# The first tile's loads, sent one kind at a time

## The chip, the cores and the metric

The kernel runs on one core of one Trainium2 chip. The metric is the device time of one execution in microseconds (us), the median of several runs. The kernel before took 1606.19 us (three runs, 1605.28 to 1607.11).

## The reference

The input is 16 sequences of 512 tokens with 256 features, in float32. Each token is normalised (`xn`), and two branches read `xn`: a linear attention with 16 heads, and a gated feed-forward network (FFN) with ternary weights. Both are added to the input.

```python
xn = layernorm(x)
# attention
q, k, v = split(xn @ W_qkv.T + b_qkv)
q, k = elu(q) + 1, elu(k) + 1
out = (q @ (k.T @ v)) / clip(q . sum(k), 1e-6)
attn = layernorm(out @ W_proj.T + b_proj) * gamma + beta + xn
# FFN, hidden width 1024; every weight is -1, 0 or 1, with one scale per row
h = silu(lin(xn, w1)) * lin(xn, w2)        # "gate" and "up"
h = gelu(lin(h, h1)); h = gelu(lin(h, h2))
return x + attn + lin(h, w3)
```

## The kernel before

A tile is one sequence, 512 tokens by 256 features. There are 16 tiles, one after the other, and all weights stay in SBUF from the first tile on. A matmul on float32 data is made of several matmuls on a high and a low part: three for the attention's weights (`three`, lines 388 to 393), two for the ternary FFN weights (`products`, line 379). The order of work on every engine is written out by hand. `over_tiles` runs `prologue` once, for what the first tile needs before its main part, then `body` for each tile; a body also does the prologue's steps for the next tile. So only the first tile's prologue has nothing beside it.

The loads ahead of the first tile are sent by three engines:

- SyncE (`sp`): the tile `x` (512 KB, line 296), then the bias of k and v (256 KB broadcast, line 326), the FFN's scales and the bias of q (`vec`, 17 KB, line 327), four more row vectors (512 KB, line 328), and then the first piece for the weight check (176 KB, line 306). The check looks at all FFN weights in 64 pieces, to learn whether they are as simple as assumed.
- ScalarE (`act`): the constants (`const`, 132 KB: an identity matrix and masks), the qkv weights (`wqkv_raw`, 768 KB), the projection's weights (`wproj_raw`, 256 KB), at lines 593 to 595.
- GpSimd (`pool`): the FFN weights in six pieces (`load_weights`, line 346). Piece 0 is gate and up (2 MB), 1 to 4 the two hidden layers (2 MB each), 5 the output layer (1 MB). Before piece 0 GpSimd waits until `x` has landed (`x_loaded`); pieces 1 to 5 follow behind the first tile's `ln1`.

The way to the first matmul with real data in the first tile is this. When `x` is there, VectorE takes its statistics (`ln1_stats`, line 708) and GpSimd computes the inverse root of the variance (`inverse_root`, line 353, one instruction). VectorE normalises (`ln1_apply`, line 714), TensorE transposes `xn` (line 401), ScalarE makes the high part (line 627) and VectorE the low part (line 727). The qkv weights are split too: ScalarE makes the high part (line 598) as soon as they have landed, and VectorE the low part (line 850), which stands behind `ln1_apply` and ahead of line 727 on VectorE. Then TensorE makes q, k and v (`q_step`, `kv_step`, lines 391 to 393) and goes on to gate and up in `body` (line 386). Before all that it does five warm-up products on zeros (line 377, ten matmuls in the profile).

ScalarE waits for `vec` after its line 598. TensorE waits for `const` before the first transposes, for `s_w[0]` at the first gate group, and for `s_w[1]` and `s_w[2]` in the first hidden group.

Of the kernel before, what the change touches and what calls it, by code (L numbers as in the profile page):

```python
# [98 lines left out]
def block_kernel(nc, H, w_ffn, w_attn, vecs, rows, consts, out):  # L99
# [70 lines left out]
    def sem(name):  # L170
        return nc.alloc_semaphore(name)
# [5 lines left out]
    s_qkv_raw = sem("qkv_weights_loaded")  # L177
# [3 lines left out]
    s_w = [sem(f"ffn_weights_loaded_{i}") for i in range(len(w_pieces))]  # L181
# [13 lines left out]
    x_loaded = Count(sem("x_loaded"), 1, unit=16)  # L195
# [77 lines left out]
    def over_tiles(eng, first, prologue, body):  # L273

        prologue(first)
        with eng.Fori(first, first + B - 1) as t:
            body(t, True)
        body(first + B - 1, False)

    def second_pass_if_needed(eng, run):  # L280
        eng.wait_ge(s_flag, 1)
        need = eng.value_load(flag[0:1, 0:1])
        with eng.If(need != 0):
            run()

    block = nc.Block()
    with block:


        @block.sync  # L290
        def _(sp):
            sp.sem_inc(acc_free.sem, 1)

            def load_x(t, first):
                sp.wait_ge(acc_made.sem, acc_made.at(t - 1, TC - 1))
                sp.dma_start(x[:], of_tile(x_dram, t - first)).then_inc(x_loaded.sem, 16)

            def of_tile(dram, tile):
                return dram[tile] if isinstance(tile, int) else dram[bass.ds(tile, 1)][0]

            def body_of(first):
                def load_piece(t, j):
                    sp.wait_ge(piece_checked.sem, piece_checked.at(t, j - 1))
                    col = (t * CHECKS + j) * CHECK_COLS
                    src = w_ffn[:, col:col + CHECK_COLS] if isinstance(col, int) else w_ffn[:, bass.ds(col, CHECK_COLS)]
                    sp.dma_start(raw[:], src.bitcast(U32)).then_inc(piece_loaded.sem, 16)

                def body(t, more):
                    if first == 0:
                        load_piece(t, 0)  # L310
                    if more:
                        load_x(t + 1, first)
                    if first == 0:
                        for j in range(1, CHECKS):
                            load_piece(t, j)
                    for half in range(2):
                        two = slice(2 * half, 2 * half + 2)
                        sp.wait_ge(out_made.sem, out_made.at(t, half))
                        sp.dma_start(of_tile(out_dram, t - first)[:, two], acc[:, two]).then_inc(out_stored.sem, 16)
                    sp.wait_ge(out_stored.sem, out_stored.at(t, 1))  # L320
                    sp.sem_inc(acc_free.sem, 1)
                return body

            def prologue(t):
                load_x(t, 0)
                sp.dma_start(rowv[:, R_BKV:], rows[:, R_BKV:].to_broadcast([P, 2 * D])).then_inc(s_bias_kv, 16)
                sp.dma_start(vec[:], vecs).then_inc(s_vec, 16)
                sp.dma_start(rowv[:, :R_BKV], rows[:, :R_BKV].to_broadcast([P, R_BKV])).then_inc(s_rows, 16)

            over_tiles(sp, 0, prologue, body_of(0))  # L330

            def second():
                sp.dma_start(w_full[:], w_ffn).then_inc(s_reload, 16)
                over_tiles(sp, B, lambda t: load_x(t, B), body_of(B))
            second_pass_if_needed(sp, second)


        @block.gpsimd
        def _(pool):
            nc.gpsimd.memset(ones[:], 1.0).then_inc(s_ones, 1)  # L340
            nc.gpsimd.memset(power[:], -0.5).then_inc(s_power, 1)
            pool.wait_ge(x_loaded.sem, x_loaded.at(0, 0))

            def load_weights(i):
                lo, hi = w_pieces[i]
                pool.dma_start(w[:, lo:hi], w_ffn[:, lo:hi]).then_inc(s_w[i], 16)

            load_weights(0)
            pool.wait_ge(s_power, 1)

            def inverse_root(t, var, done):
                pool.wait_ge(var.sem, var.at(t, 0))
                nc.gpsimd.tensor_tensor(rstd[:], vare[:], power[:], ALU.pow).then_inc(done.sem, 1)  # L353

            def ln1(t):
                inverse_root(t, ln1_var, ln1_rstd)

            def body(t, more):
                inverse_root(t, ln2_var, ln2_rstd)
                if more:  # L360
                    ln1(t + 1)

            def prologue(t):
                ln1(t)
                for i in range(1, len(w_pieces)):
                    load_weights(i)

            over_tiles(pool, 0, prologue, body)
            second_pass_if_needed(pool, lambda: over_tiles(pool, B, ln1, body))

# [219 lines left out]

        @block.scalar
        def _(act):
            act.dma_start(const[:], consts).then_inc(s_const, 16)
            act.dma_start(wqkv_raw[:].rearrange("p k n -> p (k n)"), w_attn[:, 0:DC * 3 * D]).then_inc(s_qkv_raw, 16)
            act.dma_start(wproj_raw[:].rearrange("p k n -> p (k n)"), w_attn[:, DC * 3 * D:]).then_inc(s_proj_raw, 16)
# [402 lines left out]
```

## Time and profile before

| | |
|---|---|
| median of three runs | 1606.19 us |
| span of the profiled execution, first to last instruction | 1605.2 us |
| TensorE busy with matmuls | 1591.0 us (99%) |
| VectorE busy | 945.4 us (59%) |
| ScalarE busy | 527.6 us (33%) |
| GpSimd busy | 38.1 us (2%) |

The trace comes from one execution of its own. Its span leaves out what lies around the first and the last instruction; the median of the runs is 1.0 us above it. In the profile, PE is TensorE's matmuls and PEld its weight loads, DVE is VectorE, ACT ScalarE, POOL GpSimd and SP SyncE. A name with a q behind it (ACTq) is an engine's instruction queue, which issues the transfers. L12 is line 12 of the kernel.

### The profile page before, as it was taken

Reading aid. Unit: us, or ns where it says so; the run is one execution under the profiler, and the core shown is the slowest. Engines: PE = TensorE matmul, PEld = TensorE weight load, DVE = VectorE, ACT = ScalarE, POOL = GpSimd, SP = SyncE. Lnnn points to the kernel's source line nnn. Section 1 sums busy time; section 2 is a strip of 40 time slices with the busy share of each in tenths; the row PEclk is TensorE's granted clock in tenths of the full one; section 3 lists DMA queues with packets and bytes.
Section 4 is the critical chain, followed back from the end, with each engine's and each line's share of the span. In section 5 each row is a group of like instructions: output and inputs, shape, how many; then the busy total and the mean of one; then the engine's idle time right before and its main releaser. Section 6 shows DMA issues by size and latency. Waiting matters only on the chain.

```text
span 1605.2 us, 22443 instructions
## 1 busy us (share of the span) xinstructions
PE 1591.0 (99%) x7884; PEld 1326.0 (83%) x7884; DVE 945.4 (59%) x1927; ACT 527.6 (33%) x817; POOL 38.1 (2%) x44
## 2 busy tenths in 40 slices
PE   8999999999999999999999999999999999999998
PEld 5888888888888888888888888888888888888886
DVE  5656657466564656647566474664746646566563
ACT  3324142241423424233242332423324143241421
POOL 1000000000000000000000000000000000000000
PEclk9999999999999999999999999999999999999999
DMA  9000000000000000000000000000000000000000
GB/s 355 23 12 11 27 18 22 11 11 27 18 22 18 4 27 18 22 22 0 27 18 27 18 9 18 18 27 18 18 9 18 27 18 22 11 11 27 18 10 20
DMA packets 28114, 42.07 MB, mean 26 GB/s; under 512 B 2112, under 2 KB 26816, under 8 KB 27328
## 3 DMA queue, kind: packets, MB, share of 16 engines
q1 hardware_dynamic: 26800, 29.12, 5.7%
q0 software_dynamic: 864, 11.53, 1.8%
q10 hardware_dynamic: 432, 1.18, 0.2%
q8 instruction: 10, 0.16, 0.0%
q14 instruction: 8, 0.07, 0.0%
HBM read 33.44 MB, written 8.39 MB: 26 GB/s over the span
## 4 chain that ended last, share of the span: by engine, by line
PE 99%; DMA 0%; DVE 0%; POOL 0%; issue 0%; DVEq 0%; POOLq 0%
PE ps L386 74%; PE ps L519 7%; PE ps L391 4%; PE ps L392 4%; PE ps L393 4%; PE ps L442 2%; PE ps L431 2%; PE ps L452 1%; PE ps L401 1%; DMA x<-in_H 0%; DVE wqkv_parts L850 0%; DVE xn L714 0%; DVE bn_stats L708 0%; POOL rstd L353 0%; DVE xn L837 0%
## 5 line engine op out<-in xcount | busy, mean ns | idle before, releaser
L386 PE MATMUL ps<-hidden_a,w_ffn 128*128 128x512 f32 x2048 | 488.1, 397 | 0.0
L386 PE MATMUL ps<-hidden_b,w_ffn 128*128 128x512 f32 x2048 | 484.4, 396 | 0.0
L386 PEld LDWEIGHTS ps<-hidden_b,w_ffn 128*128 128x128 f32 x2048 | 383.5, 188 | 91.6
L386 PEld LDWEIGHTS ps<-hidden_a,w_ffn 128*128 128x128 f32 x2048 | 381.4, 188 | 88.5
L622 ACT ACTIVATE value_ring<-ps,vectors 128x512 f32<-128x512 f32 x256 | 173.1, 689 | 693.7 <-PE ps L386 684.4
L386 PE MATMUL ps<-xnT,w_ffn 128*128 128x512 f32 x1024 | 249.4, 398 | 0.0
L386 PEld LDWEIGHTS ps<-xnT,w_ffn 128*128 128x128 f32 x1024 | 190.1, 188 | 43.6
L803 DVE CAST hidden_a<-value_ring 128x512 fp32r<-128x512 f32 x128 | 54.5, 426 | 216.0 <-ACT value_ring L622 216.0
L789 DVE SCALAR_TENSOR_TENSOR value_ring<-ps,vectors,gate_ring 128x512 f32<-128x512 f32 x128 | 94.2, 746 | 83.5 <-ACT gate_ring L604 83.5
L519 PEld LDWEIGHTS ps<-w_ffn,hidden_a 128*128 128x128 f32 x1024 | 123.9, 188 | 2.9
L519 PE MATMUL ps<-w_ffn,hidden_a 128*128 128x256 f32 x1024 | 124.6, 279 | 0.0
L803 DVE CAST hidden_b<-value_ring 128x512 fp32r<-128x512 f32 x128 | 54.5, 425 | 113.6 <-ACT value_ring L622 113.3
L604 ACT ACTIVATE gate_ring<-ps,vectors 128x512 f32<-128x512 f32 x128 | 86.7, 689 | 99.2 <-PE ps L386 99.0
L805 DVE TENSOR_TENSOR hidden_b<-value_ring,hidden_b 128x512 fp32r<-128x512 f32 x128 | 88.6, 692 | 4.4
L805 DVE TENSOR_TENSOR hidden_a<-value_ring,hidden_a 128x512 fp32r<-128x512 f32 x128 | 88.6, 692 | 4.4
L794 DVE TENSOR_TENSOR hidden_a<-value_ring,hidden_a 128x512 fp32r<-128x512 f32 x128 | 87.4, 683 | 2.2
L609 ACT ACTIVATE hidden_a<-value_ring 128x512 fp32r<-128x512 f32 x128 | 80.0, 625 | 9.7 <-DVE value_ring L789 9.7
L639 ACT ACTIVATE exp_tmp<-zkv 128x256 f32<-128x256 f32 x64 | 26.8, 418 | 150.1 <-DVE zkv L739 150.1
L845 DVE SCALAR_TENSOR_TENSOR low_bits<-raw_weights,low_bits 128x352 uint32<-128x352 uint32 x64 | 33.5, 523 | 68.7 <-DMA raw_weights<-in_w_ffn 68.7
L353 POOL TENSOR_TENSOR rstd<-var_plus_eps,power 128x4 f32<-128x4 f32 x32 | 34.3, 1072 | 1503.1 <-DVE var_plus_eps L703 1503.1
L739 DVE TENSOR_TENSOR zkv<-ps,row_vectors 128x512 f32<-128x512 f32 x64 | 44.3, 692 | 22.4 <-PE ps L393 22.4
L837 DVE TENSOR_TENSOR xn<-ps,row_vectors 128x512 f32<-128x512 f32 x32 | 22.1, 692 | 49.3 <-PE ps L519 49.3
(76 smaller groups left out, 1338.8 us busy)
## 6 DMA issues: line engine op xcount, KB each, us to landing
raw_weights<-in_w_ffn SPq DMA_DIRECT2D x64, 176.0 KB, 2.3
w_ffn<-in_w_ffn POOLq DMA_DIRECT2D x5, 2048.0 KB, 14.0
x<-in_H SPq DMA_DIRECT2D x16, 512.0 KB, 3.6
out_dram<-acc SPq DMA_DIRECT2D x32, 256.0 KB, 2.2
w_ffn<-in_w_ffn POOLq DMA_DIRECT2D x1, 1024.0 KB, 24.6
wqkv_raw<-in_w_attn ACTq DMA_DIRECT2D x1, 768.0 KB, 5.5
row_vectors<-in_rows SPq DMA_DIRECT2D x1, 512.0 KB, 7.8
wproj_raw<-in_w_attn ACTq DMA_DIRECT2D x1, 256.0 KB, 6.8
```

Source lines behind the costliest of these rows:

```text
L386: r = mm(bank, a, b, start=first and part == 0, stop=last and part == 1)
L391: mm(bank, wl, xh, start=first, stop=False)
L392: mm(bank, wh, xl, start=False, stop=False)
L393: return mm(bank, wh, xh, start=False, stop=last)
L519: r = mm(pair_bank(g, j)[:, 0:D], f(a) if full else a, wk, start=k == 0 and part == 0, stop=k == HC - 1 and part == 1)
L604: nc.scalar.activation(gate[:, o % 2, :], pair_bank(o, 0), ACT.Silu, scale=vec[:, V_GATE + o:V_GATE + o + 1]).then_inc(silu_made.sem, 1)
L609: nc.scalar.activation(ha[:, o, 0, :], val[:, o % 2, :], ACT.Copy).then_inc(gate_hi.sem, 1)
L622: nc.scalar.activation(val[:, n % 2, :], pair_bank(g, j), ACT.Gelu, scale=vec[:, col:col + 1]).then_inc(gelu_made.sem, 1)
L789: v.scalar_tensor_tensor(out=val[:, o % 2, :], in0=pair_bank(o, 1), scalar=vec[:, V_UP + o:V_UP + o + 1], in1=gate[:, o % 2, :], op0=ALU.m ...
L794: v.tensor_tensor(ha[:, o, 1, :], val[:, o % 2, :], ha[:, o, 0, :].bitcast(F32), ALU.subtract).then_inc(split.sem, 1)
L803: v.tensor_copy(dst[:, o, 0, :], val[:, n % 2, :]).then_inc(hid_hi.sem, 1)
L805: v.tensor_tensor(dst[:, o, 1, :], val[:, n % 2, :], dst[:, o, 0, :].bitcast(F32), ALU.subtract).then_inc(split.sem, 1)
```

## The change

Three waits are added and one is replaced. SyncE and ScalarE wait until `x` has landed before they send anything else. GpSimd waits for the qkv weights (`s_qkv_raw`) where it waited for `x`, before it sends piece 0; and it waits until piece 0 has landed before it sends pieces 1 to 5. Sizes and places of the transfers stay the same, and no computing instruction is added or moved.

```diff
             def prologue(t):
                 load_x(t, 0)
+                sp.wait_ge(x_loaded.sem, x_loaded.at(t, 0))
                 sp.dma_start(rowv[:, R_BKV:], rows[:, R_BKV:].to_broadcast([P, 2 * D])).then_inc(s_bias_kv, 16)
@@
             nc.gpsimd.memset(power[:], -0.5).then_inc(s_power, 1)
-            pool.wait_ge(x_loaded.sem, x_loaded.at(0, 0))
+            pool.wait_ge(s_qkv_raw, 16)
@@
             def prologue(t):
                 ln1(t)
+                pool.wait_ge(s_w[0], 16)
                 for i in range(1, len(w_pieces)):
                     load_weights(i)
@@
         def _(act):
+            act.wait_ge(x_loaded.sem, x_loaded.at(0, 0))
             act.dma_start(const[:], consts).then_inc(s_const, 16)
```

## Rows read from the trace of the kernel before

**Rows 1.** The page: the span, and TensorE's share.
```profile
span 1605.2 us, 22443 instructions
PE 1591.0 (99%) x7884; PEld 1326.0 (83%) x7884; DVE 945.4 (59%) x1927; ACT 527.6 (33%) x817; POOL 38.1 (2%) x44
```

**Rows 2.** Who waited for whom, whole span: us in total, times, longest.
```profile
PE ps L401 <- DVE xn L714: 3.8, 1, 3.8
...
PE ps L377 <- DVE value_ring L691: 2.6, 1, 2.6
...
PE ps L391 <- DVE xnT L727: 1.1, 1, 1.1
```

**Rows 3.** The chain that ended last, 0 to 47 us: start, us, what.
```profile
1.20 7.40 DMA x<-in_H
...
10.83 0.10 issue
10.93 1.04 POOL rstd L353
12.00 1.38 DVE xn L714 x4
13.38 1.67 DVE wqkv_parts L850
15.05 0.66 DVE xnT L727
...
15.84 0.76 PE ps L391
...
21.30 0.43 PE ps L391
...
21.97 0.23 PE ps L393
```

**Rows 4.** The timeline, 0 to 28 us: start, us, instruction, idle before.
```profile
0.75 0.39 ACTq L593 DMA_DIRECT2D constants<-in_consts  x1
...
1.18 0.45 ACTq L594 DMA_DIRECT2D wqkv_raw<-in_w_attn  x1
...
1.69 0.51 SPq L326 DMA_DIRECT2D row_vectors<-in_rows  x1
...
6.67 1.48 ACT L598 ACTIVATE wqkv_parts<-wqkv_raw 128x1536 fp32r<-128x1536 f32 x1 [3.17 <-DMA wqkv_raw<-in_w_attn]
...
8.70 1.40 DVE L708 BATCH_NORM_STATS2 bn_stats<-x 128x6 f32<-128x256 f32 x4 [5.82 <-DMA x<-in_H]
...
8.90 0.71 POOL L346 DMA_DIRECT2D w_ffn<-in_w_ffn  x1 [8.01 <-DMA x<-in_H]
...
11.94 2.83 POOL L346 DMA_DIRECT2D w_ffn<-in_w_ffn  x5
```

**Rows 5.** Transfers, whole span: size each, median us from issue to landing.
```profile
x<-in_H SPq DMA_DIRECT2D x16, 512.0 KB, 3.6
...
w_ffn<-in_w_ffn POOLq DMA_DIRECT2D x1, 1024.0 KB, 24.6
wqkv_raw<-in_w_attn ACTq DMA_DIRECT2D x1, 768.0 KB, 5.5
row_vectors<-in_rows SPq DMA_DIRECT2D x1, 512.0 KB, 7.8
...
constants<-in_consts ACTq DMA_DIRECT2D x1, 132.0 KB, 2.3
```

**Rows 6.** The same view, 8.5 to 10 us: piece 0 alone.
```profile
w_ffn<-in_w_ffn POOLq DMA_DIRECT2D x1, 2048.0 KB, 7.8
```

**Rows 7.** The timeline again: the first users of the other loads.
```profile
14.37 1.08 ACT L627 ACTIVATE xnT<-ps 128x512 fp32r<-128x512 f32 x2 [6.22 <-PE ps L401]
...
27.00 3.89 PE L386 MATMUL ps<-xnT,w_ffn 128*128 128x512 f32 x16
...
45.47 7.71 PE L386 MATMUL ps<-hidden_a,w_ffn 128*128 128x512 f32 x32
```

## The prediction

> **What bounds the kernel now.** I read the page first. TensorE is busy for 1591.0 of 1605.2 us [rows 1], so it is idle for 14.2 us in all, and only time before its first real product, idle time, or time at its lower clock can be gained by sending loads otherwise. The view of who waited for whom, over the whole span, has three waits of TensorE that are not weight loads: 2.6 us before the warm-up, 3.8 us for `xn` and 1.1 us for the low part of `xnT` [rows 2]. All three lie before 16 us. No wait of TensorE on a transfer is in that list: gate and up, the hidden layers and the output layer were each there when they were wanted. So as long as none of them comes late now, the change can only matter through the stretch up to 15.84 us, where the first q product starts [rows 3]. From there TensorE runs without a gap until its last product, and whatever shifts this start shifts the end.
>
> The chain of waits shows what sets the 15.84 [rows 3]. `x` is issued at 1.20 and lands at 8.60. VectorE's statistics end at 10.78 (after them stands 0.10 of issue, at 10.83), GpSimd's inverse root runs from 10.93, the normalising from 12.00, the low part of the qkv weights from 13.38, the low part of `xnT` from 15.05 to 15.71, and TensorE starts 0.13 later. The reader is to see that `x` is the late transfer here, and that the qkv weights are not: issued at 1.18 [rows 4], they took 5.5 us [rows 5] and were there at 6.7, when ScalarE took them up [rows 4], long before VectorE came to them at 13.38.
>
> **`x` alone.** The first `x` took 7.40 us [rows 3], beside the constants, the attention's weights and the row vectors. The median of all 16 `x` loads is 3.6 us [rows 5], and 15 of them meet almost no traffic. With nothing else sent, `x` should land at 1.20 + 3.6 = 4.8, some 3.8 us sooner. The statistics need 8.70 to 10.83, so they would end near 7.0. If that were all, the start of q would move up by 3.8 us.
>
> **The qkv weights behind `x`.** They can no longer overlap with it. ScalarE resumes when `x` is there: the lag from landing to first instruction was 0.10 us on VectorE (8.60 to 8.70) and 0.30 on GpSimd (to 8.90) [rows 3, 4]; I take 0.1. The constants' issue is first, and the weights' issue starts 0.43 after it (0.75 to 1.18) [rows 4]: 4.8 + 0.1 + 0.43 = 5.35. For the transfer I take its own row, 5.5 us [rows 5]. They had `x` (512 KB) and the row vectors beside them then, and will have the two row vectors (256 and 512 KB), `vec` and the check's first piece beside them now, so it is the nearest case. Landing: 10.9, where it was 6.7. The bounds are wide. Below, a smaller transfer with little beside it, `x` at 3.6, gives 9.0. Above, the 512 KB of row vectors that took 7.8 us in the crowd [rows 5] give 13.2.
>
> **GpSimd's wait for the qkv weights.** This is the step that decides. The inverse root of the first tile stands behind piece 0 on GpSimd, and piece 0 now waits for the qkv weights. Before, GpSimd was through with its issue (8.90 + 0.71 = 9.61) before the variance was there [rows 4]. Now the variance is ready at 7.0 and lies there until the weights have landed. Call that landing T. Then: lag 0.3, issue 0.71 [rows 4], 0.10 to the next instruction, taken from the row of issue [rows 3]: the inverse root starts at T + 1.1. From its start to the start of q the chain has 15.84 - 10.93 = 4.91 us of steps that stay as they are [rows 3]: the root, normalising, both low parts. So q starts at T + 6.0. It starts as before if T is 9.8. With T = 10.9 it starts at 16.9, that is 1.1 us later than 15.84. At the bounds: 15.0 (0.8 sooner) and 19.2 (3.4 later). The gain on `x` is given away in full, for the reason that everything behind GpSimd's wait starts with the qkv weights.
>
> ScalarE's high part of the weights takes 1.48 us from T [rows 4], and is done when VectorE wants it, at T + 1.1 + (13.38 - 10.93) = T + 3.55. That step hides, and with it a table load of ScalarE if that should fall behind the same wait.
>
> A rule that bears on this: the Trainium skill, in DMA: Bandwidth & Descriptors (Anatomy of one DMA, SWDGE path), gives a transfer from GpSimd as about 2.0 us plus its bytes over 436 GB/s. That would be 3.8 us for 768 KB, and by it T would be 9.2 and q would start 0.6 us sooner than before. The `x` row agrees roughly, since the rule gives 3.2 us and the trace has 3.6 [rows 5]; these two transfers are sent by other engines, though, and the weights are not alone. It is the case of the first rival below.
>
> **SyncE's wait.** Queued behind it are the k and v bias, `vec`, the other row vectors and the check's first piece. The bias now goes at 4.9 instead of 1.69, everything behind it by the same 3.2 us. The slowest of this group took 7.8 us [rows 5]. So `vec`, issued near 5.5 (the bias' issue takes 0.51 [rows 4]), is there by 13.3; ScalarE wants it before its line 627, at 14.37 [rows 7] and now at 15.4. The bias is there by 12.7 and wanted behind the q products, which start after 15.0 even at the lower bound; the rest is wanted later still in VectorE's order. The constants, sent at 4.9 and 2.3 us on the way [rows 5], are wanted by the transposes near 14.7. Cost nothing, with 2.1 us of cover for `vec` at the least. The cover shrinks if T is early: at T = 9.0 ScalarE wants `vec` at 13.5.
>
> **Piece 0.** It is issued at 11.2 instead of 8.90. Its row has 7.8 us [rows 6], with less beside it now, since pieces 1 to 5 are held back: landing by 19.0. TensorE wants it at 27.00 [rows 7], now 28.1. Cost nothing, 9 us of cover.
>
> **GpSimd's wait for piece 0.** The five issues start at 19.3 instead of 11.94 [rows 4]. Behind them on GpSimd stands only the inverse root of the second layernorm, which follows the first hidden groups. The last of the five was issued at 11.94 + 2.83 - 0.55 = 14.2 and landed 24.6 us later [rows 4, 5], at 38.8, so 26.9 after the first issue, and part of that was spent on piece 0. So all five are in by 46.2. The first hidden group wants only piece 1, at 45.47 [rows 7] and now 46.6. Cost nothing.
>
> **The clock.** TensorE's matmuls of 512 columns come every 0.43 us until 21.30 and every 0.23 from 21.97 [rows 3]: the lower and the higher level, 1.2 and 2.4 GHz. The rise came 5.8 us after the start of q. The clock is down because of the idle time before, and that gap of 3.8 us [rows 2] only grows, so nothing more is lost there. If the rise follows the work, the delay of 1.1 us stays whole. If it comes at the same moment as before, 2.5 matmuls that would have run at the lower level run at the higher one, and the delay is 2.5 x 0.23 = 0.6. If it came later still, each us would add about 0.5 us. The Trainium skill, in TensorE: Matmul & The Clock Gate (the HAM clock gate), says that the monitor runs freely and does not start with the kernel, so that the moment of rise differs from run to run. By that rule the mean delay over many runs is the whole 1.1; one trace can't show it.
>
> **Sum.** `x` 3.8 sooner; the weights and GpSimd's wait turn that into a start 1.1 us later; everything else hides. The profiled execution would go from 1605.2 to 1606.3. The median lies 1.0 above the span, so I forecast 1606.19 + 1.1 = 1607.3. About 0.2% (3.2 us) is what a measurement of this kernel can tell from no change; this is a third of it.
>
> **The rivals.**
>
> 1. The qkv weights come faster than their old row, since `x` is no longer beside them, T = 9.0 to 9.8. For it: `x` was sent at the same time as they were (1.20 and 1.18 [rows 3, 4]) and is twice the size of the bias that is sent at their side now. Against: the row vectors are sent at the same moment. Time: 0.8 us sooner, 1605.4. Chance 0.2.
>
> 2. The row vectors take more from the weights than `x` did, being sent together with the constants, ahead of the weights. T = 12 to 13.2, 2.2 to 3.4 later, 1608.4 to 1609.6. Chance 0.12. Against it: the weights came through ahead of their neighbours before (5.5 against 7.8 us for fewer bytes [rows 5]).
>
> 3. The first `x` is slow of itself (start of the queue, first access), and not because of its neighbours: it lands at 8.6 as before, and the weights follow. ScalarE sends them at 9.15, T is 14.65, q starts at 20.7, 4.8 us later: 1611.0. It is slower by over 0.2% from T = 13.0 on, so from a landing of `x` at 6.9. For it speaks that the first `x` has the longest time of the 16. Against it, the constants, sent before it, landed in 2.3 us [rows 5], so the start costs less than that. Chance 0.05.
>
> 4. Piece 0 becomes the wait, because its place in the order is later. It would have to take 16.9 us and took 7.8 [rows 6]. If it took the 24.6 of the last piece, TensorE would stand for 7.7 us more: 1615. Chance 0.02.
>
> 5. The waits act otherwise than the diff says, for example the start stays where it was: 1606.2. Chance 0.03.
>
> **Chances and range.** The forecast (T from 9.8 to 12, a delay of 0 to 2.2 us) has 0.58, the rivals 0.2, 0.12, 0.05, 0.02 and 0.03. The forecast and rival 2 up to 1609.2 and most of rival 1 make 8 in 10, with the three runs of before themselves 1.8 us apart; the range is 1605.0 to 1609.2. Slower by over 0.2% are rivals 3 and 4 and the end of rival 2: 0.08. Faster by over 0.2% would need T = 6.6, which not even the lower bound gives: 0.01. Within: 0.91.
>
> **What would show it.** In the profile of the changed kernel: `x` lands near 4.8 (right) or later than 6.9 (rival 3). The qkv weights land near 10.9, with GpSimd's wait before line 346 put down to them and not to `x`. The inverse root starts 1.1 us behind that landing, though its input is ready near 7.0. The q product starts near 16.9. Pieces 1 to 5 are issued after 18, and the list of TensorE's waits has no transfer in it. The clock's rise is at 21 to 23. The forecast is wrong if q starts before 15.8, if a wait of TensorE on `w_ffn` shows, or if `vec` or the constants end ScalarE's or TensorE's wait.

## The result, and the profile after

The changed kernel took 1608.95 us (median of 18 runs, 1607.81 to 1610.32), the kernel before 1605.81 us (18 runs, 1604.43 to 1607.11) beside it. The ratio is 1.002, with a 95% interval of 1.0013 to 1.0027: 3.1 us slower, and some 2.1 to 4.3 by the interval. I had forecast 1.1 us slower. The direction and the part of GpSimd's wait were right; the qkv weights took 2.1 us longer than I had taken them to. The size was nearly three times what I gave, and lies at the edge of the 0.2% that I had called hard to tell from nothing. In the experiments below two executions of the kernel before took 2633 and 4067 us, and no ratio counts them.

The page after. TensorE's busy time has grown by 0.7 us, and the clock's mean in the first slice is lower; the other 2.2 of the 2.9 us of span are time in which TensorE stands still.

```profile
span 1608.1 us, 22443 instructions
PE 1591.7 (99%) x7884; PEld 1326.7 (82%) x7884; DVE 945.5 (59%) x1927; ACT 527.3 (33%) x817; POOL 38.0 (2%) x44
```

The chain that ended last, 0 to 34 us (start, us, what). It answers to [rows 3].

```profile
1.19 3.32 DMA x<-in_H
4.54 0.39 ACTq L596
4.96 7.56 DMA wqkv_raw<-in_w_attn
...
13.64 1.05 POOL rstd L354
14.72 1.39 DVE xn L717 x4
16.11 0.25 issue
16.36 1.10 PE ps L403 x4
17.55 0.61 ACT xnT L630
18.18 0.70 DVE xnT L730
18.88 0.14 issue
19.02 0.76 PE ps L393
...
24.47 0.39 PE ps L393
24.86 0.24 PE ps L394
```

The reader is to see three things. `x` lands at 4.51 instead of 8.60. The chain then leaves `x` and runs through the qkv weights, which take 7.56 us, and from them over GpSimd to the inverse root. And the chain has changed its members behind the root: where it went through the low part of the weights on VectorE, it now goes through the transposes (line 403), ScalarE and then VectorE. q starts at 19.02 instead of 15.84, 3.2 us later.

The waits, whole span (us in total, times, longest), against [rows 2]: VectorE now waits 8.0 us for the root, whose input has been ready since 6.7.

```profile
POOL w_ffn L347 <- DMA wqkv_raw<-in_w_attn: 11.9, 1, 11.9
...
DVE xn L717 <- POOL rstd L354: 8.0, 1, 8.0
...
PE ps L403 <- DVE xn L717: 6.7, 1, 6.7
```

The transfers in the first 110 us (size, median us to landing) answer to [rows 5]. The constants take 5.2 us where they took 2.3.

```profile
wqkv_raw<-in_w_attn ACTq DMA_DIRECT2D x1, 768.0 KB, 7.6
...
row_vectors<-in_rows SPq DMA_DIRECT2D x1, 256.0 KB, 4.8
...
constants<-in_consts ACTq DMA_DIRECT2D x1, 132.0 KB, 5.2
```

From the start of q on nothing differs up to the last computing instruction: gate and up start at 30.17 instead of 27.00, and VectorE's last instruction ends at 1603.19 instead of 1600.02, both 3.2 us later. The spans differ by 2.9, so 0.3 us is made up behind that, where only the output is still being stored.

### The profile page after: what moved, and what is told of

It reads as the page before. It is cut to its first block, busy times and chain, and to the rows that moved or that the text cites. A ratio compares the mean times of both kernels' runs of the same rounds, so it can differ in the third digit from the quotient of the medians.

```text
span 1608.1 us, 22443 instructions
## 1 busy us (share of the span) xinstructions
PE 1591.7 (99%) x7884; PEld 1326.7 (82%) x7884; DVE 945.5 (59%) x1927; ACT 527.3 (33%) x817; POOL 38.0 (2%) x44
## 4 chain that ended last, share of the span: by engine, by line
PE 98%; DMA 1%; DVE 0%; issue 0%; POOL 0%; ACT 0%; ACTq 0%; DVEq 0%; POOLq 0%
PE ps L388 74%; PE ps L521 7%; PE ps L393 4%; PE ps L394 4%; PE ps L395 4%; PE ps L444 2%; PE ps L433 2%; PE ps L454 1%; PE ps L403 1%; DMA wqkv_raw<-in_w_attn 0%; DMA x<-in_H 0%; DVE xn L717 0%; POOL rstd L354 0%; DVE xnT L730 0%; DVE xn L840 0%
```

## Experiments

Twelve kernels were run; the question was why the qkv weights take 7.6 us, and what of the loss is GpSimd's order. The times of most are within a few us of each other, and single executions of the kernel before differ by more than 2 us, so for the runs with one execution I read the trace and draw nothing from the time. In the table, "consts" and "weights" are us from issue to landing, "landed" and "q" the moments at which the qkv weights were there and the first q product started. The kernels with a ratio were timed against the kernel before in several rounds. There is one trace of each kernel. Where the loads beside the weights are the same, the weights' time repeats: 7.56, 7.51 in the changed kernel and e2, and 4.45, 4.34 and 4.50 in e1, e3 and e8.

| kernel | consts | weights | landed | q | ratio to before (95%) |
|---|---|---|---|---|---|
| before | 2.3 | 5.5 | 6.7 | 15.84 | |
| changed | 5.2 | 7.56 | 12.52 | 19.02 | 1.002 (1.0013 to 1.0027) |
| e1 rows behind weights | 2.3 | 4.45 | 9.43 | 15.47 | 0.9996 (0.9987 to 1.0005) |
| e2 root first | 5.1 | 7.51 | 12.56 | 16.60 | 1.0003 (0.9994 to 1.0012) |
| e3 both | 2.2 | 4.34 | 9.47 | 13.52 | 0.998 (0.9971 to 0.9989) |
| e4 spread rows of the weights first | 5.1 | 6.90 | 11.85 | 18.35 | |
| e5 even 256 KB of H first | 3.0 | 7.25 | 12.29 | 18.79 | |
| e6 512 KB behind | 5.4 | 7.42 | 12.57 | 19.07 | |
| e7 bias behind | 2.3 | 6.03 | 11.13 | 17.63 | |
| e8 both, and filler | 2.2 | 4.50 | 9.63 | 13.68 | 0.9974 (0.9963 to 0.9984) |
| e9 only 256 KB of H beside | 3.2 | 5.08 | 10.11 | 16.61 | |
| e10 only one row of H beside | 4.5 | 6.00 | 11.16 | 17.65 | |
| e11 SyncE's and ScalarE's waits alone | 5.0 | 8.82 | 13.99 | 18.04 | 1.0017 (1.0007 to 1.0027) |
| e12 GpSimd's waits alone | 2.2 | 5.7 | 6.9 | 16.48 | 1.0004 (0.9994 to 1.0014) |

### The two costs taken out one by one (e1, e2, e3)

The edit of e1 to the changed kernel, on SyncE:

```diff
                 sp.wait_ge(x_loaded.sem, x_loaded.at(t, 0))
-                sp.dma_start(rowv[:, R_BKV:], ...)   # the bias
                 sp.dma_start(vec[:], vecs).then_inc(s_vec, 16)
+                sp.wait_ge(s_qkv_raw, 16)
+                sp.dma_start(rowv[:, R_BKV:], ...)
```

> SyncE sends `vec` behind `x`, and everything else only when the qkv weights have landed. All else as in the changed kernel. Theory A (the 256 KB bias, one row of 2 KB read for all 128 partitions, holds the DMA engines while the constants and the qkv weights stand behind it): the constants land in under 3 us, the qkv weights in about 4.5 us instead of 7.6, near 9.5; q starts at that landing + 6.0 to 6.5, near 15.5 to 16; 3 us faster than the changed kernel, level with the kernel before (1605.8, +-0.7). Theory B (a load that is sent after a wait is slow of itself, the queue has to start again): the qkv weights still take over 7 us, q starts near 19, 1609.

Its chain, 0 to 24 us:

```profile
1.19 3.34 DMA x<-in_H
...
4.98 4.45 DMA wqkv_raw<-in_w_attn
...
10.55 1.05 POOL rstd L355
...
15.47 0.77 PE ps L394
```

The weights took 4.45 us and landed where theory A had them; theory B, that a load sent after a wait is slow of itself, is out. q starts 3.5 us sooner than in the changed kernel, and the kernel is level with the one before. So taking away what SyncE sends beside the weights is enough to win back what was lost. It is not the only way: e2, next, comes back to the same level without it.

The edit of e2 to the changed kernel, on GpSimd:

```diff
-            pool.wait_ge(s_qkv_raw, 16)
-            load_weights(0)
@@ prologue
                 ln1(t)
+                pool.wait_ge(s_qkv_raw, 16)
+                load_weights(0)
                 pool.wait_ge(s_w[0], 16)
```

> GpSimd does the first inverse root before it waits for the qkv weights and sends piece 0. All else as in the changed kernel. Theory A: the root starts near 6.7 instead of 13.6; the qkv weights land at 12.5 as before; from there the high part 1.5, the low part 1.7, the low part of xnT 0.7, so q starts near 16.6, 2.4 us sooner than in the changed kernel: 1606.6. The transposes run right behind the warm-up, at the higher clock. Rival: the order on GpSimd costs nothing, since the weights' split sets the start anyway: q near 19, 1609.

Its chain. The root is gone from it, and the weights' own split sets the start:

```profile
5.05 7.51 DMA wqkv_raw<-in_w_attn
...
12.59 1.49 ACT wqkv_parts L601
...
14.10 1.76 DVE wqkv_parts L853
15.86 0.61 DVE xnT L730
...
16.60 0.76 PE ps L393
```

With the weights as slow as in the changed kernel, q starts 2.4 us sooner, at 16.60 as expected to the tenth. GpSimd's order alone costs those 2.4 us, 4.0 us from landing to q against 6.5.

e3 has both edits.

> Both edits together: SyncE's rows behind the qkv weights, and GpSimd's root first. Theory A: weights land near 9.5, q starts 4.0 us later, near 13.5, over 2 us sooner than in the kernel before: 1603.5, and less if the clock is still high. Rival: `vec` comes late (ScalarE waits for it ahead of the high part of xnT) or something else now ends last, and q starts near 15 to 16: 1605 to 1606. Theory B: q near 16.5, 1606.5.

q started at 13.52, and the median was 1603.3 us against 1606.42 of the kernel before: a real gain, whose interval reaches from 1.8 to 4.7 us. So the plan of the change, `x` first and the rest in the order of need, does pay once the row vectors stand behind the weights and the root ahead of the wait.

### What SyncE's loads do to the weights (e4 to e7, e9, e10)

First, 256 KB from 128 rows of the attention's weights were put in the bias' place, with the bias behind `vec`. They land in `acc`, so SyncE now declares `acc` free only when they are there; those lines are left out here and in the next edits shown:

```diff
+                sp.dma_start(acc[:]...[:, 0:2 * D], w_attn[:, 0:2 * D]).then_inc(s_probe, 16)
                 sp.dma_start(vec[:], vecs).then_inc(s_vec, 16)
                 sp.dma_start(rowv[:, R_BKV:], ...)   # the bias
```

> The changed kernel with a load added where the bias stood: 256 KB from 128 different rows of HBM, packets of 2 KB as the bias has, into a tile that is not in use yet; `vec` and the bias follow. So 256 KB more are sent, and nothing else changes. Theory A (it is the one row read for all that is slow): the added load's packets take about 0.08 us each instead of 0.19, the constants land in 2.5 to 3.5 us instead of 5.2, and the qkv weights in 6 to 7 us, unless the bias holds them up from its new place. Rival (any 256 KB sent ahead costs the same): constants 5.2 and weights 7.6 us or more.

The constants still took 5.1 us. Per queue and us, the first line is all packets, q1 is SyncE's queue and q10 ScalarE's (packets, MB, share of 16 engines). The changed kernel, 6 to 7 us, and e4:

```profile
DMA packets 86, 0.15 MB, mean 150 GB/s; under 512 B 0, under 2 KB 26, under 8 KB 86
q1 hardware_dynamic: 60, 0.12, 73.8%
q10 hardware_dynamic: 26, 0.03, 10.6%
```

```profile
DMA packets 100, 0.17 MB, mean 171 GB/s; under 512 B 0, under 2 KB 34, under 8 KB 100
q1 hardware_dynamic: 66, 0.14, 78.3%
q10 hardware_dynamic: 34, 0.04, 23.1%
```

SyncE's 60 packets held the engines for 73.8% of 16 us, 0.20 us each; e4's 66 for 0.19 each. (The time of a packet does not repeat as well as the rate: e6 below sends the same bias first, and its 61 packets in this microsecond held the engines for 44.6%, 0.12 us each, at the same 148 GB/s in all.) So spread rows were as slow as the one row, and theory A as I had put it failed this test. These rows lie 8 KB apart and are read by the weights' own transfer too, however, so the next kernel took 256 KB of H in one piece.

```diff
-                sp.dma_start(acc[:]...[:, 0:2 * D], w_attn[:, 0:2 * D]).then_inc(s_probe, 16)
+                sp.dma_start(acc[:]...[:, 0:2 * D], H[1], first half, two tokens to a row).then_inc(s_probe, 16)
```

> As the run with 256 KB of spread rows in the bias' place, but these come from 256 KB of H that lie in one piece, so that they share no rows and no pitch with the qkv weights. In that run the first packets of 2 KB took as long (66 packets, 78.3% of 16 engines in 1 us: 0.19 us each) as the bias' (0.20 us), which speaks against theory A. If the slow start there came from the place of the source (rows of w_attn, 8 KB apart, read by the weights too), the packets now take near 0.09 us, the constants land in 2.5 to 3.5 us and the weights in under 6.3 us. If it is theory C (whatever SyncE sends at the same moment as ScalarE's constants slows them, by its bytes and at the start of both queues), the constants take 5 us and the weights near 7 again.

```profile
DMA packets 227, 0.32 MB, mean 323 GB/s; under 512 B 17, under 2 KB 125, under 8 KB 227
q1 hardware_dynamic: 116, 0.21, 64.7%
q10 hardware_dynamic: 111, 0.11, 32.8%
```

In the same microsecond, 6 to 7, twice the bytes moved, at 0.09 us a packet, and the constants landed in 3.0 us. So the slow start is a matter of the source and not of the two queues starting together. The weights still took 7.25 us, which neither side had expected: the bias, now third in its queue, was under way from 9 us on, and the rate fell to 228 GB/s from 9 to 10 us, from 332 in the microsecond ahead of it. The slow stretch had moved with the bias.

e6 and e7 then took away one of SyncE's two large loads each. e6 waits for the weights ahead of the 512 KB, e7 sends the 512 KB early and waits ahead of the bias. In both, as in e1, the 176 KB of the weight check fall behind the weights too.

> The changed kernel with SyncE's wait for the qkv weights put ahead of the 512 KB of row vectors alone; the bias and `vec` stay beside them. Bytes: 0.5 MB of rows and 0.18 MB of the check's piece no longer share the engines. At 0.39 MB/us (9 to 12.5 us of the changed kernel) that is up to 1.7 us: theory C has the constants at 5 us still, the weights at 6.0 to 6.5 us. If the whole loss comes from the start with the bias, the weights stay at 7.5; if it comes from the 512 KB alone, they take 4.5 us and the constants 2.3.

> The reverse: `vec` and the 512 KB stay beside the qkv weights, and the bias and the check's piece go behind them. Theory C: the 512 KB start with packets of 4 KB in the bias' place, so the constants take 4 to 5 us and the weights near 6.5 to 7. If the small packets of the bias alone make the slow start, the constants land in under 3 us and the weights in near 5.5.

With the bias beside them and not the 512 KB, the weights took 7.42 us; with the 512 KB and not the bias, 6.03. Against the 4.45 us of e1, with neither, the smaller load costs 3.0 us and the load of twice its size 1.6. Together, and with the check's piece, they cost 3.1: the weights of the changed kernel are slow mainly because of the bias. Theory C, which counts bytes, is wrong for both: 6.0 to 6.5 was expected for e6, and 6.5 to 7 for e7, whose constants landed in 2.3 us and not in 4 to 5.

The last pair leaves only 256 KB beside the weights. The source is the one difference between the two:

```diff
-   H[1:2].rearrange("o (h p two) d -> p (o h) (two d)", h=2, two=2)[:, 0]                # e9: 256 KB in one piece
+   H[1:2].rearrange("o (r two) d -> (o r) (two d)", two=2)[0:1].to_broadcast([P, 2 * D])  # e10: 2 KB, read 128 times
```

> Only 256 KB of H in one piece (in the bias' place, 2 KB packets) and `vec` go beside the constants and the qkv weights; the bias and the 512 KB follow when the weights have landed. With the bias itself in this place the weights took 7.4 us, with nothing but `vec` 4.5. If it is the bytes, 0.26 MB at 0.39 MB/us: 5.1 us at most. If any transfer from SyncE in this place costs what the bias did (the two queues starting together): 7.4.

> The same kernel, but the 256 KB are one row of 2 KB of H, read 128 times, as the bias is read from its row. If reading one row for all partitions is what is slow: the weights take 7.4 us as beside the bias, the constants 5, and the rate from 6 to 8 us is 120 to 160 GB/s. If it is something about the bias' own place in memory: 5.1 us as beside the even 256 KB.

The queues from 7 to 8 us, e9 and then e10:

```profile
DMA packets 261, 0.43 MB, mean 429 GB/s; under 512 B 164, under 2 KB 197, under 8 KB 261
q10 hardware_dynamic: 108, 0.40, 100.4%
q1 hardware_dynamic: 153, 0.03, 14.5%
```

```profile
DMA packets 157, 0.17 MB, mean 171 GB/s; under 512 B 58, under 2 KB 116, under 8 KB 157
q1 hardware_dynamic: 88, 0.08, 50.3%
q10 hardware_dynamic: 69, 0.09, 26.4%
```

256 even KB cost the weights 0.6 us (5.08 against 4.45), which is about what their bytes cost (0.26 MB at the 0.39 MB/us of the changed kernel from 9 to 12.5 us, 0.7 us). The same bytes from one row cost 1.5 us, at 161 and 171 GB/s from 6 to 8 us against 313 and 429. So reading one row for all partitions is slow, at the start at least. It explains 0.9 us of the 2.3 that the bias costs beyond its bytes (7.42 less 5.08); the other 1.4 us belong to something in the bias' own place or form that I have not found.

Two traces say more about "at the start". In e1 the bias is sent when the weights are in. From 10 to 12 us only SyncE's queue moves anything, first the bias and then the 512 KB, at 100 GB/s in the first microsecond and 197 in the second. In the changed kernel `x`, alone as well, ran at 171 GB/s from 2 to 3 us and 349 from 3 to 4. The two stretches of e1:

```profile
q1 hardware_dynamic: 49, 0.10, 28.6%
...
q1 hardware_dynamic: 86, 0.20, 73.3%
```

So the bias starts slowly with nothing beside it. In the kernel before it was not slow at all. It stood behind `x` in the queue and was issued some 5 us ahead of its turn; from 7.5 to 8 us, with all but a few KB of `x` moved, SyncE's queue moved 0.18 MB and the engines 375 GB/s in all:

```profile
q1 hardware_dynamic: 132, 0.18, 104.0%
```

So one row read for all is not slow wherever it stands. It was slow in the first 2 us of a load that had nothing of its queue right ahead of it. Why is not shown: an early issue is not enough, since the bias of e5 was issued at 5.48, 3.5 us ahead of its first packets, and the rate fell all the same.

### The parts of the change alone (e11, e12)

e11 is the kernel before with the two waits of SyncE and ScalarE, e12 the kernel before with the two edits on GpSimd.

> The kernel before with SyncE's and ScalarE's wait for `x` alone; GpSimd sends piece 0 when `x` is there, does the root and sends pieces 1 to 5 at once, as before. The root starts near 7 us, so it holds nobody. The qkv weights now have the bias and GpSimd's 16 KB packets beside them: they land at 13 to 15 us, and q starts 4.0 us after that, at 17 to 19: 1607.4 to 1609.4. If GpSimd's packets take little from them, 12.5 and 16.5: 1606.9.

> The kernel before with GpSimd's two edits alone: piece 0 waits for the qkv weights (which land at 6.7) instead of `x` (8.6), and pieces 1 to 5 for piece 0. The root is not held up, since its input comes later than the weights. q starts at 15.8, or some tenths later if piece 0, sent near 7, slows `x`. No measurable difference: 1606.4, +-0.8.

e11's loss (1.0017) cannot be told from that of the whole change, and comes another way: without GpSimd's waits the 16 KB packets of the FFN weights stand beside the qkv weights, which land at 13.99 instead of 12.52, but the root is not held up, and q starts 4.0 us after them, 1.0 us sooner than in the changed kernel. GpSimd's wait for the weights saves 1.5 us of transfer and costs 2.4 by the root behind it. e12 shows no difference that can be measured, as expected. In its trace q starts at 16.48, 0.6 late: `x` lands 0.2 later, and the transposes ran at the lower clock.

### Keeping TensorE busy up to q (e8)

```diff
                     transposes(t, 1)
                     if not full:
+                        for i in range(3):
+                            mm(pair_bank(0, 0), val[:, 0, 0:P], val[:, 1, :], start=True, stop=True)
                         pe.wait_ge(s_wqkv, 1)
```

> The kernel with both edits, and three more products on zeros on TensorE between the first transposes and the wait for the split weights. There TensorE stood idle for 2.7 us, the clock fell behind that, and some ten products ran at 0.43 instead of 0.23 us. Theory: TensorE is busy until just before q starts, the clock stays at its higher level, q still starts near 13.5 and gate and up start 2.0 us sooner: 1601.3. Rival: the filler ends behind the weights' split and pushes the start by as much as it saves, or the clock falls all the same: 1603.3.

The chains of e3 and of e8, q products behind the start:

```profile
13.52 0.47 PE ps L394
13.99 0.33 PE ps L395
14.31 0.43 PE ps L396
```

```profile
13.68 0.47 PE ps L394
...
14.38 0.23 PE ps L396
...
15.07 0.23 PE ps L396
```

In e3 the clock fell to its lower level at about 14.2 us, behind an idle stretch of 2.7 us, and the products came every 0.43 us up to 17.3. In e8 they came every 0.23 us throughout; gate and up start at 22.41 us instead of 23.78 in e3, 1.4 us sooner of the 2.0 expected; q itself began 0.16 later in this trace. The median was 1602.03 us, the span 1600.2 against 1601.9. Against the kernel before this is the fastest kernel of the study, 1.6 to 3.7 permille faster; that it is faster than e3 too rests on the traces, since the intervals of the two overlap.

## Why the prediction was right in sign and short in size

The median lies inside the range that I gave, but that was in part luck. The forecast itself had a delay of 0 to 2.2 us, and the delay was 3.2; what lets 1608.95 fall below my upper bound of 1609.2 is the room I had left for rival 2, and that the kernel before came out at 1605.81 over 18 runs, 0.4 us below the 1606.19 that I had added to. The parts:

- **What bounds the kernel** held. The kernels with a ratio are slower or faster as q starts later or sooner than 15.84 (e3 and e8 below 14, e11 and the changed kernel at 18 and above, the rest level), and in no trace does TensorE wait for an FFN piece.
- **`x` alone** held: landed at 4.51 (4.8 forecast), variance ready at 6.69 (7.0).
- **The qkv weights behind `x`** failed, in the sentence "For the transfer I take its own row, 5.5 us ... so it is the nearest case". Measured 7.56, landing at 12.52 instead of 10.9. The row was not the nearest case, because I counted neighbours by what had been issued and not by what was ahead in each queue. Before, the bias stood in SyncE's queue behind `x`, and `x` has 0.52 MB. The queues of the kernel before show that SyncE's had moved 0.42 MB in 406 packets by 6.6 us, when the weights landed. These are packets of 1 KB, those of `x`, and not the 2 KB of the bias, so the bias had hardly begun:

```profile
q10 hardware_dynamic: 194, 0.52, 89.7%
q1 hardware_dynamic: 20, 0.02, 2.9%
...
q10 hardware_dynamic: 126, 0.48, 52.2%
q1 hardware_dynamic: 386, 0.40, 44.8%
```

  These are the stretches 2 to 4 us and 4 to 6.6 us. Besides being wanted, `x` screened the weights from the row vectors, and holding everything for `x` took the screen away. This was my second rival (12 to 13.2 us, 2.2 to 3.4 us later), to which I gave 0.12. It was put down to bytes and to the place ahead of the weights; e6 and e9 show that the larger part is not the bytes (7.42 us beside 256 KB of bias, 5.08 beside 256 even KB). No run has ScalarE's wait without SyncE's, so which of the two took the screen away is not shown; with the bias sent right behind `x`, as before, the weights might have lost less.
- **GpSimd's wait** held: root at T + 1.12 (1.1 forecast), and e2 shows that taking it out of the way gives 2.4 us back.
- **From the root to q** was 0.5 us short: 5.38 us instead of 4.91. "The clock is down because of the idle time before, and that gap only grows, so nothing more is lost there" was wrong. [rows 2] has a gap of 3.8 us before the first transposes, and they still ran at the higher level behind it. The gap is now 6.7 us and they ran at the lower one: the eight took 1.94 us, and 1.06 in the trace of before. That put the transposes into the chain in place of the weights' low part. The two rows, before and after; the granted clock was 1.00 from 13.6 to 14.8 us before, and 0.50 from 16.3 to 18.4 after:

```profile
13.64 1.06 PE L401 MATMUL ps<-constants,xn 128*128 128x128 f32 x8 [3.84 <-DVE xn L714]
...
16.36 1.94 PE L403 MATMUL ps<-constants,xn 128*128 128x128 f32 x8 [6.74 <-DVE xn L717]
```

  Of this row I had read only the level at q, not at the transposes.
- **The clock behind q.** The rise came at about 24.7 us, 5.7 after the start of q, where it had been 5.8: in this pair it followed the work, and the delay stayed whole. Elsewhere it did not: in e1, where q started at 15.47, the rise came at about 21.6, 6.1 after it, and in e2 3.7 after it. These are traces of different kernels; but the 18 runs of the changed kernel have mean granted clocks from 0.995 to 0.998, and the one at 0.998 has the shortest span, 1605.9 us of 1605.9 to 1608.4. The Trainium skill, in TensorE: Matmul & The Clock Gate (What's actually happening), says that the moment of the rise differs from run to run; these runs agree.
- **SyncE's wait, piece 0, GpSimd's wait for piece 0** held nobody up, as argued: what they delay was there when it was wanted. But that was only half of the question for SyncE's wait: I had asked who waits for its rows, and not what they would slow down by starting together with the weights. That cost is in the weights' 2.1 us above. Piece 0 was issued at 12.81 and was in by 20.5, with 9.7 us of cover; the list of TensorE's waits has no transfer in it.
- **Rival 1** (weights faster than their old row) is what e1 and e3 show with the rows out of the way: 4.45 and 4.34 us. **Rivals 3 to 5** are out by `x` at 4.51, piece 0 in 7.7 us and the start at 19.02.

The sum, with the trace's terms: weights 2.1 us slower than taken, `x` and the issue 0.4 sooner, transposes 0.5 later. 1.1 + 2.1 - 0.4 + 0.5 = 3.3, against 3.2 measured at q.

## What to carry to other kernels

A load that is sent early can be screened by what stands ahead of its rivals in their own queue, as the qkv weights were here: 5.5 us with the bias behind `x`, 7.56 with the bias sent beside them. Before holding a queue back, list for each transfer what would then start in the same moment, by queue order and not by issue time. And an instruction that issues a transfer behind a wait holds everything on its engine: look for short computing steps behind it, and put them ahead.

## What the runs showed of the hardware that I had not expected

- 256 KB read from one row of 2 KB for 128 partitions and issued next to a transfer of 768 KB cost it 3.0 us (bias) or 1.5 us (a row of H), and 256 even KB 0.6 us. The engines moved 117 to 171 GB/s from 6 to 8 us with one row, 313 and 429 with even data. 256 KB from rows 8 KB apart were slow as well (171 and 153 GB/s).
- The same bias was slow with nothing beside it (100 GB/s from 10 to 11 us in e1), and was not where it followed `x` in its queue (375 GB/s in all from 7.5 to 8 us in the kernel before).
- The 512 KB of row vectors, with 4 KB to a row and also read for all partitions, cost only 1.6 us. Why the smaller row is the dearer one stays open.
- TensorE's clock outlasted 3.8 us without work before the transposes in the kernel before, and had fallen after 4.8 us in e12 and 6.7 us in the changed kernel. In e3 it fell only behind the start of q.
